# One change in three stages of a twelve-stage decoder: order of the expert choice, engine of the rounding, layout of the head transfers

## The chip, the cores and the metric

The kernel runs on one core of a Trainium2 chip, as one program. The metric is device time in microseconds (us). TensorE multiplies matrices, VectorE and ScalarE work elementwise, GpSimd does so too, SyncE issues the transfers between memory (HBM) and the on-chip SBUF; TensorE's results lie in PSUM. Each engine works through its own queue in order and waits for others on semaphores.

## The reference, cut to what matters

The residual `x` (2 batches of 512 tokens, 256 features) passes through twelve sublayers, each `x = x + f(layernorm(x))`. The change touches three of them:

```python
# L0_ffn: six experts e, 100 low-rank tokens each; every input token takes one expert
logits = x @ w_gate;  gates = one_hot(argmax(logits))          # top-1, softmax of one value = 1
attn   = softmax(x @ tokens[e].T / 16)                         # per expert, over its 100 tokens
delta  = ((attn[:, :, 1:] @ val[e, 1:] + x) @ wd_w.T + wd_b) * scale
out    = log(sum_e exp(delta) * gates)                         # 0 replaced by float32 eps

# L1_ffn: both matrix products on values rounded to whole numbers
q(x) = round(x / s),  s = max(|x|.max(), 1e-6) / 127
h = gelu((q(x) @ q(w1).T + b1) * s_x * s_w1);   out = (q(h) @ q(w2).T + b2) * s_h * s_w2

# L2_xattn: 16 heads of 16 features, 512 queries, 1024 keys per batch
p = softmax(q @ k.T / 4 + (1 - mask) * -1e9) * group_prob;   out = (p @ v) @ wo + bo
```

## The kernel before

Activations lie feature-major: 256 features as two chunks of 128 partitions, 1024 tokens along the free dimension. `decoder` calls the stages one after another with a fence between them: every engine's queue must be drained before the next stage starts. Within a stage the order on each engine is written out by hand in functions `tensor`, `scalar`, `vector`, `gpsimd` and `sync`, and a `Signal` is a semaphore count (`x(n)`: the n-th event of that name). `k.beat` (L157) issues filler matmuls whose results nobody reads.

**`l0_ffn`** (L701). Six value blocks are computed (L745, L846) and row 0 of `val` is cleared (L848), which leaves token 0 out. Then come eight tiles of 128 tokens. For a tile TensorE computes the scores of all six experts and the gate logits into one of two PSUM slots (L758). VectorE takes the maxima and finds the one chosen expert, ties by rank (L856 to L868); ScalarE does six exponentials with sums (L812); VectorE divides by the sum and by the choice (L870 to L874: reciprocal, times choice, times the 128x600 probabilities); TensorE transposes six blocks (L772) and ScalarE copies them out (L817). TensorE's order is: logits of tile `it`, then transposes of tile `it - 1`; for `it = 8` in place of logits the mixing of the first half (`mix`, L789). After the tiles follow `blend` (L889), `close` (L797) and `finish` (L896 to L901) per half. GpSimd adds the normed input to the residual once per half (L906).

**`l1_ffn`** (L1380). After eight GELUs (L1440) VectorE has eight per-partition maxima; `Quantizer` reduces them on VectorE (L1157), over the partitions by a GpSimd all-reduce (L1161), and forms scale and inverse (L1165, L1167). Rounding is by adding and subtracting 1.5 times 2 to the 23rd: the multiplication with the addition is on VectorE (L1478, a ring of four buffers), the subtraction, which also converts to bf16, on VectorE for even and on GpSimd for odd blocks (L1486, L1502). TensorE multiplies block by block (L1425), behind 12 filler matmuls. GpSimd adds the bias to the residual (L1506) and VectorE the scaled product (L1491).

**`l2_xattn`** (L1846). Queries and keys are split into three bf16 parts of falling size, and the score is one matmul with 96 rows: six products of parts times 16 features (L1989). A chunk of 128 features x 512 tokens (8 heads) is computed (L1951), split (L2070, L2074, L2153, L2255, L2157) and stored to a scratch tensor (L1915); `fetch` brings a head back with its 96 rows. The first six chunks have a buffer each; the six later ones, of heads 8 to 15, are made during the head loop and share one buffer, so ScalarE's split waits until the chunk before is stored. Before the loop SyncE issues: mask and group probabilities of batch 0 (2 MB each), chunks 0 to 2, a wait, head 0 for batch 0, chunks 3 to 5, a wait, head 0 for batch 1, mask and group of batch 1, head 1. The loop has 128 tiles (head, batch, 128 queries), four per head and batch, software-pipelined over steps: score, masked sum with negation and minimum (L2219), exponential (L2111), transposes (L2000), weighting by the group probabilities (L2231 and L2267), product with the values (L2011, L2015). ScalarE turns the integer mask into a float bias (L2080) in one operation per batch, that of batch 1 ahead of the exponential of tile 2.

```python
sp.dma_start(qs[z][blk * dh:(blk + n) * dh, q],
             scr_q[head][:, 0:n, q].rearrange("f j t -> j f t")).then_inc(*done.up())   # n = 3, 2, 1
```

Of the kernel before, what the change touches and what calls it, by code (L numbers as in the profile page):

```python
# [7 lines left out]
ACT = mybir.ActivationFunctionType  # L8
# [9 lines left out]
P = 128  # L18
# [682 lines left out]
def l0_ffn(k):  # L701
# [22 lines left out]
    (x_early,) = k.signals("pool", 1)  # L724

    def tensor(pe):
# [20 lines left out]
        for it in range(TILES + 1):  # L747
# [13 lines left out]
            else:  # L761
                pe.wait_ge(*exped(6 * TILES - 6))
                mix(pe, 0)
# [72 lines left out]
    def vector(dve):  # L836
# [10 lines left out]
        dve.wait_ge(*value_out(E_))  # L847
        dve.memset(val[0:1], 0.0).then_inc(*value_out.up())  # L848
        ln.scale(dve, 1)
        for it in range(TILES):  # L850
            ps, s, p = k.slot(2 + it % 2), sm[it % 2], prob3[it % 2]
            mx, ng, su, gr = s[:, 0:7], s[:, 8:14], s[:, 16:22], s[:, 24:30]
            eq, m2, rs = s[:, 32:38], s[:, 40:41], s[:, 48:54]
            gl = ps[:, S + L_:S + L_ + E_]
            dve.wait_ge(*logit(it + 1))
            dve.tensor_reduce(mx[:, 0:5], ps[:, 0:500].rearrange("p (e l) -> p e l", e=5), AX.X,  # L856
                              OP.max).then_inc(*pick.up())
            dve.tensor_reduce(mx[:, 5:6], ps[:, S:S + L_], AX.X, OP.max).then_inc(*pick.up())
            dve.tensor_reduce(mx[:, 6:7], gl, AX.X, OP.max).then_inc(*pick.up())
            dve.wait_ge(*pick(8 * it + 3))  # L860
            dve.tensor_scalar(ng, mx[:, 0:6], -1.0 / 16, None, OP.mult).then_inc(*pick.up())
            dve.tensor_scalar(eq, gl, mx[:, 6:7], None, OP.is_equal).then_inc(*pick.up())
            dve.wait_ge(*pick(8 * it + 5))
            dve.tensor_tensor(eq, eq, rank, OP.mult).then_inc(*pick.up())
            dve.wait_ge(*pick(8 * it + 6))
            dve.tensor_reduce(m2, eq, AX.X, OP.max).then_inc(*pick.up())
            dve.wait_ge(*pick(8 * it + 7))
            dve.tensor_scalar(eq, eq, m2, None, OP.is_equal).then_inc(*pick.up())  # L868
            dve.wait_ge(*exped(6 * it + 6))
            dve.reciprocal(rs, su).then_inc(*weighed.up())  # L870
            dve.wait_ge(*weighed(3 * it + 1))
            dve.tensor_tensor(gr, rs, eq, OP.mult).then_inc(*weighed.up())
            dve.wait_ge(*weighed(3 * it + 2))
            dve.tensor_tensor(p, p, gr.unsqueeze(2).broadcast_to([P, E_, L_]), OP.mult).then_inc(*weighed.up())  # L874
            if it == TILES - 1:
                blend(dve, 0)
# [7 lines left out]
        if nxt:  # L884
            nxt.scale(dve, 0)

# [16 lines left out]
    def gpsimd(pool):  # L903
        for h in range(B):
            pool.wait_ge(*ln.out(h + 1))
            pool.tensor_tensor(k.X[:, :, half(h)], k.X[:, :, half(h)], k.Hn[:, :, half(h)], OP.add).then_inc(*x_early.up())  # L906
# [473 lines left out]
def l1_ffn(k):  # L1380
# [17 lines left out]
    up, down = k.signals("pe", 2)  # L1398
    (gelu,) = k.signals("act", 1)
    bias1, largest, whole, scaled1, bias2, scaled, rounded_dve, resid = k.signals("dve", 8)  # L1400
    rounded_pool, x_early = k.signals("pool", 2)
# [3 lines left out]
    on_pool = lambda kt: kt % 2 == 1  # L1405
    rounded = lambda kt: (rounded_pool if on_pool(kt) else rounded_dve)(kt // 2 + 1)
# [4 lines left out]
    def tensor(pe):  # L1411
# [8 lines left out]
        k.beat(k.slot(2)[:, 0:S], 12)  # L1420
# [12 lines left out]
    def scalar(act):  # L1433
# [8 lines left out]
        act.preload_act_table_set(LN_EXP)  # L1442
        if nxt:
            nxt.square(act, 0)

    def vector(dve):
        ln.open_vector(dve)
# [25 lines left out]
        hid_q.scale(dve)  # L1473
        for kt in range(FC + 1):
# [9 lines left out]
            if kt and not on_pool(kt - 1):  # L1484
                dve.wait_ge(*scaled(kt))
                dve.tensor_scalar(hidq[:, kt - 1, :], tmp2(kt - 1), ROUND, None, OP.subtract).then_inc(*rounded_dve.up())  # L1486
# [10 lines left out]
    def gpsimd(pool):  # L1497
        in_q.gpsimd(pool)
        hid_q.gpsimd(pool)
        for kt in range(1, FC, 2):  # L1500
            pool.wait_ge(*scaled(kt + 1))
            pool.tensor_scalar(hidq[:, kt, :], tmp2(kt), 1.0, -ROUND, OP.mult, OP.add).then_inc(*rounded_pool.up())  # L1502
            if kt == 1:
                pool.wait_ge(*bias2(2))
            if kt in (1, 3):
                pool.tensor_scalar(k.X[:, kt // 2, :], k.X[:, kt // 2, :], 1.0, b2s[:, kt // 2:kt // 2 + 1], OP.mult,  # L1506
                                   OP.add).then_inc(*x_early.up())
# [338 lines left out]
def l2_xattn(k):  # L1846
    a, w, name, dh = k.a, k.work, "L2_xattn", 16
    NK, nk, keys, ROWS = B * S2, S2 // P, S2, 96
    scr_q = k.nc.dram_tensor("parts_q_" + name, (H, dh, 3, NT), BF16, kind="Internal").ap()
    scr_k = k.nc.dram_tensor("parts_k_" + name, (H, dh, 3, NK), BF16, kind="Internal").ap()  # L1850
# [27 lines left out]
    RING = (0, 1, 2, 4, 6)  # L1878
    count = lambda x, which: sum(ch[0] == which for ch in CHUNKS[:x])
# [23 lines left out]
    def fetch(sp, head, q, t, done):  # L1903
        z = head % 2
# [13 lines left out]
    def sync(sp):  # L1918
# [17 lines left out]
        for head in range(2, H):  # L1936
# [3 lines left out]
            if head == 8:  # L1940
                sp.wait_ge(*stored(len(CHUNKS)))
# [1480 lines left out]
```

## Time and profile before

| | us |
|---|---|
| median of 3 runs | 1848.98 (1846.49 to 1850.38) |
| profiled execution | 1846.75 |
| its span | 1845.4 |
| mean granted TensorE clock | 0.971 |

| engine | busy us | share |
|---|---|---|
| TensorE | 1658.8 | 90% |
| VectorE | 1052.5 | 57% |
| ScalarE | 905.1 | 49% |
| GpSimd | 428.8 | 23% |

The span is that of one profiled execution; times in the rows are microseconds from its start. On that scale `l0_ffn` lies at about 268 to 363, `l1_ffn` at 590 to 643 and `l2_xattn` at 985 to 1340. PE is TensorE, DVE VectorE, ACT ScalarE, POOL GpSimd, SP SyncE. L874 is line 874 of the kernel. A clock of 1.00 is 2.4 GHz and 0.50 is 1.2 GHz.

### The profile page before, as it was taken

The numbers are of one execution on the slowest core, as the hardware profiler recorded it, in microseconds if no ns is written. First come the engines' busy times: TensorE is split into PE (matmuls) and PEld (weight loads), VectorE is DVE, ScalarE is ACT, GpSimd is POOL, SyncE is SP. The second block draws the span as 40 slices with busy tenths as digits, with TensorE's granted clock in tenths as the row PEclk, the third lists the DMA queues.
The fourth block names the chain that finished last, engine by engine and source line by source line (L and its number), as shares of the span: only waits on it lengthen the run. The fifth ranks groups of instructions, "written<-read, shape, count | busy, mean of one in ns | idle before, by whom it ended". The sixth has DMA issues, their size and how long they took to land. (4 is left out here: it accounts for less than half of the span.)

```text
span 1845.4 us, 22986 instructions
## 1 busy us (share of the span) xinstructions
PE 1658.8 (90%) x7762; PEld 854.0 (46%) x7762; DVE 1052.5 (57%) x2163; ACT 905.1 (49%) x1762; POOL 428.8 (23%) x534
## 2 busy tenths in 40 slices
PE   7899997988998788999989689999988889999997
PEld 2334444434665234434335455566534444555545
DVE  4731115484322749889845578888737634655525
ACT  2331213352333247777833578878732563555523
POOL 0010000000000225555511345555601011232300
PEclk9999998999999899999999799999999899999999
DMA  5000100001000000000104311010116402000000
GB/s 220 1 0 0 40 0 1 33 2 46 1 1 17 1 9 9 18 10 10 50 1 149 132 52 51 33 37 29 31 41 178 132 8 85 21 11 21 1 1 23
DMA packets 31844, 69.42 MB, mean 38 GB/s; under 512 B 4213, under 2 KB 18357, under 8 KB 30293
## 3 DMA queue, kind: packets, MB, share of 16 engines
q1 hardware_dynamic: 31728, 67.95, 11.4%
q8 instruction: 63, 1.03, 0.2%
q14 instruction: 53, 0.43, 0.1%
HBM read 55.78 MB, written 12.06 MB: 37 GB/s over the span
## 5 line engine op out<-in xcount | busy, mean ns | idle before, releaser
L2267 POOL TENSOR_TENSOR work<-work,arena_a 128x512 f32<-128x512 f32 x128 | 167.9, 1312 | 155.8 <-ACT work L2129 155.5
L2000 PE MATMUL ps<-identity,ctx_keys 128*128 128x128 f32 x1024 | 144.9, 281 | 17.0 <-ACT work L2129 14.5
L2219 DVE CUSTOM_DVE_ANT_0 ctx_keys<-ps,arena_b 128x1024 f32<-128x1024 f32 x128 | 154.9, 1212 | 6.7 <-ACT arena_b L2080 6.2
L2000 PEld LDWEIGHTS ps<-identity,ctx_keys 128*128 128x128 f32 x1024 | 118.8, 144 | 65.3 <-ACT work L2129 21.3
L2111 ACT ACTIVATE ctx_keys<-ctx_keys,small 128x1024 f32<-128x1024 f32 x128 | 146.9, 1147 | 0.7 <-DVE small L2219 0.7
L2231 DVE TENSOR_TENSOR work<-ps,arena_a 128x512 f32<-128x512 f32 x128 | 88.0, 688 | 46.2 <-PE ps L2000 39.1
L3113 POOL TENSOR_SCALAR ctx_keys<-ctx_keys,small 128x128 f32<-128x128 f32 (+3 forms) x128 | 66.9, 535 | 172.6 <-DVE small L3036 172.6
L2129 ACT ACTIVATE work<-ps 128x512 f32<-128x512 f32 x128 | 76.3, 596 | 62.0 <-PE ps L2000 58.7
L1802 POOL TENSOR_SCALAR work<-work 128x1024 f32<-128x1024 int32 x64 | 66.6, 1040 | 112.7 <-DVE work L1755 112.3
L339 PE MATMUL ps<-work,arena_a 128*128 128x512 f32 x192 | 85.1, 595 | 7.9 <-DVE work L515 3.2
L1989 PE MATMUL ps<-work 96*128 96x512 bf16 x256 | 79.3, 393 | 14.2 <-DMA work<-parts_k_L_xattn 9.4
L214 ACT ACTIVATE norm_parts<-normed 128x1024 f32<-128x1024 f32 x24 | 25.3, 1054 | 129.2 <-DVE normed L207 129.2
L1601 PE MATMUL ps<-work 64*128 64x512 f32 x256 | 73.2, 648 | 16.7 <-DVE work L1755 14.5
L157 PE MATMUL ps<-identity 128*128 128x512 bf16 x320 | 79.5, 399 | 7.9 <-DVE normed L237 2.9
L2988 ACT ACTIVATE ctx_keys<-ctx_keys,small 128x128 f32<-128x128 f32 (+3 forms) x128 | 70.7, 553 | 29.1 <-DVE small L3028 28.7
L1755 DVE SCALAR_TENSOR_TENSOR work<-work,ps 128x1024 int32<-128x1024 f32 x64 | 78.0, 1218 | 12.2 <-ACT work L1693 12.1
L1738 DVE TENSOR_SCALAR work<-work,small 128x512 int16<-128x512 f32 x128 | 81.0, 674 | 2.3
L1677 ACT ACTIVATE work<-work 128x512 f32<-128x512 f32 x128 | 80.3, 644 | 2.4 <-POOL work L1802 2.4
L1161 POOL PARTITION_ALL_REDUCE small<-small x4 | 1.4, 358 | 328.7 <-DVE small L1157 328.7
L3062 DVE COPY work<-ps 128x128 f32<-128x128 f32 (+1 forms) x64 | 31.3, 489 | 75.7 <-PE ps L2904 75.2
L1625 PE MATMUL ps<-arena_a,work 128*64 128x512 f32 x256 | 66.3, 622 | 1.6 <-DVE work L1773 1.5
L1647 PE MATMUL ps<-normed,head_weights 128*128 128x512 f32 x128 | 63.7, 620 | 3.8 <-DVE work L1746 3.0
(389 smaller groups left out, 3417.3 us busy)
## 6 DMA issues: line engine op xcount, KB each, us to landing
arena_b<-in_mask SPq DMA_DIRECT2D x2, 2048.0 KB, 8.8
arena_a<-in_groupT SPq DMA_DIRECT2D x2, 2048.0 KB, 14.8
head_weights<-in_w_L_xattn SPq DMA_DIRECT2D x8, 449.0 KB, 3.3
arena_a<-in_w_l_attn SPq DMA_DIRECT2D x1, 3072.0 KB, 14.6
head_weights<-in_w_L_attn SPq DMA_DIRECT2D x8, 384.0 KB, 3.0
work<-parts_q_L_attn SPq DMA_DIRECT2D x8, 384.0 KB, 4.7
work<-parts_k_L_attn SPq DMA_DIRECT2D x8, 384.0 KB, 5.1
work<-parts_k_L_xattn SPq DMA_DIRECT2D x15, 192.0 KB
```

The source lines that it names most:

```text
L157: self.pe.matmul(bank, ib[:, 0:P], ib.unsqueeze(1).broadcast_to([P, 2, 2 * P]), start=True, stop=True)
L339: mm = pe.matmul(k.bank(i), wT[:, c, m * P:(m + 1) * P], src[:, c, :], start=c == 0, stop=c == DC - 1)
L1677: op = act.activation(ex[i % NE][:, h, :], ex[i % NE][:, h, :], ACT.Exp, scale=1.0 / FX, accum_out=sums[i % 4][:, h:h + 1])
L1738: op = dve.tensor_scalar(attn[i % 2][:, h * S:(h + 1) * S], ex[i % NE][:, h, :], recip[i % 4][:, h:h + 1], OFFSET - HALF, OP.mult, OP.add)
L1755: dve.scalar_tensor_tensor(out=score[i % NS], in0=sign[i % 2], scalar=-HALF, in1=s_bank[i % 2], op0=OP.mult, op1=OP.add).then_inc(*truncat ...
L1989: mm = pe.matmul(s_psum[i % NS][:, o:o + S], qs[h][0:ROWS, q0:q0 + P], ks[h][0:ROWS, b * keys + o:b * keys + o + S], start=True, stop=True)
L2000: mm = pe.transpose(t_psum[z][:, kt * P:(kt + 1) * P], prob[i % NP][:, o:o + P], k.iden[:, :])
L2111: act.activation(p, p, ACT.Exp, scale=-1.0, bias=minmax[:, i % 8:i % 8 + 1], accum_out=sums[:, i % 8:i % 8 + 1]).then_inc(*exped.up())
L2129: act.activation(PT[i // 4 % 2][:, 4:8, i % 4 * P:(i % 4 + 1) * P], t_psum[1].rearrange("p (k t) -> p k t", t=P), ACT.Copy).then_inc(*turn ...
L2219: dve.tensor_tensor_reduce(prob[i % NP], s_psum[i % NS], NEG[:, b, qt, :], -1.0, BIG * 3e8, OP.add, OP.min, minmax[:, i % 8:i % 8 + 1]).th ...
L2231: dve.tensor_tensor(PT[i // 4 % 2][:, 0:4, qt * P:(qt + 1) * P], t_psum[0].rearrange("p (k t) -> p k t", t=P), GT[:, b, 0:4, qt * P:(qt + ...
L2267: pool.tensor_tensor(p, p, GT[:, b, 4:8, qt * P:(qt + 1) * P], OP.mult).then_inc(*weighed_pool.up())
```

## The change

In `l0_ffn` the loop on VectorE is split into `choose` and `weigh`; `choose` of a tile is issued before `weigh` of the tile before, the second scale of the layernorm comes after the first `choose`, and the memset of the values' first row moves to GpSimd, between its two additions. TensorE waits for that memset before its first mixing; else its order is the same.

```diff
-        dve.wait_ge(*value_out(E_))
-        dve.memset(val[0:1], 0.0).then_inc(*value_out.up())
-        ln.scale(dve, 1)
-        for it in range(TILES):
...
+        for it in range(TILES + 1):
+            if it < TILES:
+                choose(dve, it)
+            if it == 0:
+                ln.scale(dve, 1)
+            if it:
+                weigh(dve, it - 1)
+        blend(dve, 0)
```

`choose` holds the operations L856 to L868, with the negation (L861) ahead of the gate's maximum (L859) and a wait of its own; `weigh` holds L870 to L874.

In `l1_ffn` the maximum over the partitions of the second quantization goes through TensorE: a transposition of the 128x1 maxima to one row, a reduction on VectorE, a matmul with a row of ones that brings it back to all partitions. Of the eight subtractions ScalarE gets six (blocks 1 to 3 and 5 to 7) and VectorE two; GpSimd keeps the two bias additions alone.

```diff
-        k.beat(k.slot(2)[:, 0:S], 12)
+        pe.wait_ge(*fixed(2))
+        k.beat(k.slot(2)[:, 0:S], 6)
+        pe.wait_ge(*hid_q.done(1))
+        pe.transpose(k.slot(0)[0:1, 0:P], hid_q.am, k.iden[:, :]).then_inc(*peak.up())
+        pe.wait_ge(*hid_q.done(2))
+        pe.matmul(k.slot(1)[:, 0:1], ones, top, start=True, stop=True).then_inc(*peak.up())
+        k.beat(k.slot(2)[:, 0:S], 5)
...
+        for kt in range(FC):
+            if on_act(kt):
+                act.wait_ge(*scaled(kt + 1))
+                act.activation(hidq[:, kt, :], tmp2(kt), ACT.Identity, bias=unround).then_inc(*rounded_act.up())
```

In `l2_xattn` the scratch tensors hold the six blocks of 128 partitions already repeated, with the features of the eight heads interleaved (the weights are laid out so on the host). A chunk is stored in three transfers, which together write six blocks; a head is fetched in two transfers of 96 rows each. The mask of batch 1 is turned in four pieces, at steps 3 to 6, ahead of the exponentials of tiles 1 to 4, and each masked sum waits for its own piece.

```diff
-        for blk, n in ((0, 3), (3, 2), (5, 1)):
-            sp.dma_start(qs[z][blk * dh:(blk + n) * dh, q],
-                         scr_q[head][:, 0:n, q].rearrange("f j t -> j f t")).then_inc(*done.up())
...
+        for dst, scr, tokens in ((qs, scr_q, q), (ks, scr_k, t)):
+            sp.dma_start(dst[z][0:ROWS, tokens],
+                         scr[m].rearrange("j (f h) t -> (j f) h t", h=8)[:, h, tokens]).then_inc(*done.up())
...
+    PIECES = {"q": (range(0, 3), range(0, 2), range(0, 1)), "k": ((0, 0, 0), (1, 1), (2,))}
+        for block in PIECES[which]:
+            n, j = len(block), block[0]
+            src = parts[x][:, 0:n, :] if which == "q" else parts[x][:, j:j + 1, :].broadcast_to([P, n, S])
+            sp.dma_start(scr[row:row + n, :, t0:t0 + S].rearrange("j p t -> p j t"), src).then_inc(*stored.up())
+            row += n
...
-            if step == 4:
-                mask(1)
+            if 3 <= step < 7:
+                mask(1, slice(step - 3, step - 2))
```

## Rows read from the trace of the kernel before

**Rows 1.** The page's busy times: us, share of the span, instructions.
```profile
PE 1658.8 (90%) x7762; PEld 854.0 (46%) x7762; DVE 1052.5 (57%) x2163; ACT 905.1 (49%) x1762; POOL 428.8 (23%) x534
```
**Rows 2.** Order of time, VectorE, one tile of `l0_ffn`: start, duration, operation.
```profile
304.34 0.67 DVE L856 TENSOR_REDUCE small<-ps 128x5 f32<-128x500 f32 x1
...
306.01 0.23 DVE L868 TENSOR_SCALAR small<-small 128x6 f32<-128x6 f32 x1
308.37 0.19 DVE L870 RECIPROCAL small<-small 128x6 f32<-128x6 f32 x1 [2.13 <-ACT work L812]
...
308.80 0.78 DVE L874 TENSOR_TENSOR work<-work,small 128x600 f32<-128x600 f32 x1
309.50 0.67 DVE L856 TENSOR_REDUCE small<-ps 128x5 f32<-128x500 f32 x1
```
**Rows 3.** Order of time, TensorE in `l0_ffn`: transposes, logits, mixing.
```profile
294.25 1.49 PE L772 MATMUL ps<-identity,work 128*100 128x128 f32 x6 [5.80 <-DVE work L874]
...
305.24 2.27 PE L758 MATMUL ps<-arena_b,normed 128*128 128x500 f32 x8
309.72 0.83 PE L772 MATMUL ps<-identity,work 128*100 128x128 f32 x6 [2.22 <-DVE work L874]
310.39 3.87 PE L758 MATMUL ps<-arena_b,normed 128*128 128x500 f32 x8
...
325.87 10.46 PE L789 MATMUL ps<-work,arena_b 100*128 100x512 f32 x24
```
**Rows 4.** Order of time around the first tile of `l0_ffn`, GpSimd and VectorE.
```profile
287.62 2.34 POOL L906 TENSOR_TENSOR resid<-resid,normed 128x1024 f32<-128x1024 f32 x1 [14.31 <-DVE normed L237]
...
288.40 1.58 DVE L861 TENSOR_SCALAR small<-small 128x6 f32<-128x6 f32 x1
...
293.32 0.78 DVE L874 TENSOR_TENSOR work<-work,small 128x600 f32<-128x600 f32 x1
```
**Rows 5.** Stretch, length, busy us of the five engines, granted clock, DMA share, GB/s.
```profile
309.50:314.70 5.20, 4.54 (x14) 2.60 (x14) 2.87 (x13) 2.76 (x13) 0.00 (x0) 0.67 0.02 5
```
**Rows 6.** Order of time in `l1_ffn` from the last GELU to the residual.
```profile
618.14 4.40 PE L157 MATMUL ps<-identity 128*128 128x512 bf16 x12 [2.45 <-ACT work L1440]
...
620.56 1.42 DVE L1478 TENSOR_SCALAR arena_b<-work,small 128x1024 f32<-128x1024 f32 x2
...
627.93 1.03 POOL L1502 TENSOR_SCALAR work<-arena_b 128x1024 bf16<-128x1024 f32 x1 [7.79 <-issue]
...
630.55 1.52 DVE L1486 TENSOR_SCALAR work<-arena_b 128x1024 bf16<-128x1024 f32 x1
...
635.12 1.41 POOL L1502 TENSOR_SCALAR work<-arena_b 128x1024 bf16<-128x1024 f32 x1 [0.64 <-DVE arena_b L1478]
...
637.32 2.73 DVE L1491 SCALAR_TENSOR_TENSOR resid<-ps,small,resid 128x512 f32<-128x512 f32 x4 [1.68 <-PE ps L1425]
```
**Rows 7.** The page's groups, ScalarE on 128x1024: busy us, mean ns.
```profile
L1693 ACT ACTIVATE work<-ps 128x1024 f32<-128x1024 f32 x64 | 65.7, 1026 | 0.0
```
**Rows 8.** Order of time at the start of `l2_xattn`'s loop: SyncE, ScalarE, TensorE.
```profile
1014.36 1.91 SPq L1906 DMA_DIRECT2D work<-parts_q_L_xattn  x3
...
1018.20 0.41 SPq L1922 DMA_DIRECT2D arena_b<-in_mask  x1
...
1028.19 3.71 ACT L2080 ACTIVATE arena_b<-arena_b,small 128x4096 f32<-128x4096 int32 x1 [10.88 <-DMA arena_b<-in_mask]
...
1041.81 1.03 PE L1989 MATMUL ps<-work 96*128 96x512 bf16 x2 [2.86 <-DMA work<-parts_k_L_xattn]
...
1045.08 1.14 ACT L2111 ACTIVATE ctx_keys<-ctx_keys,small 128x1024 f32<-128x1024 f32 x1
```
**Rows 9.** Stretches as in Rows 5: masks in flight, then a head's fetch alone.
```profile
1024.00:1027.00 3.00, 3.00 (x13) 2.44 (x12) 0.69 (x1) 0.00 (x0) 0.00 (x0) 0.50 1.02 403
1036.00:1039.00 3.00, 2.95 (x16) 2.17 (x14) 2.36 (x6) 2.16 (x5) 1.73 (x2) 0.68 0.17 68
```
**Rows 10.** Waits in `l2_xattn`: who for whom, us in total, times, longest.
```profile
ACT head_weights L2074 <- DMA parts_k_L_xattn<-head_weights: 0.8, 1, 0.8
```

More of the change, by code:

```diff
@@ L1397, in l1_ffn @@
     in_q, hid_q = Quantizer(k, view(k.small, 8, 4)), Quantizer(k, view(k.small, 12, 4))
-    up, down = k.signals("pe", 2)
-    (gelu,) = k.signals("act", 1)
+    up, down, peak = k.signals("pe", 3)
+    gelu, rounded_act = k.signals("act", 2)
     bias1, largest, whole, scaled1, bias2, scaled, rounded_dve, resid = k.signals("dve", 8)
-    rounded_pool, x_early = k.signals("pool", 2)
+    (x_early,) = k.signals("pool", 1)
+    (fixed,) = k.signals("dve", 1)
+    ones, top, unround = view(w, 0, P)[0:1], view(k.small, 17, 1)[0:1], view(k.small, 16, 1)
     hv = hq.rearrange("p (c t) -> p c t", c=2)
@@ L1446, in vector @@
     def vector(dve):
+        dve.memset(unround, -ROUND).then_inc(*fixed.up())
+        dve.memset(ones, 1.0).then_inc(*fixed.up())
         ln.open_vector(dve)
@@ L1472, in vector @@
         hid_q.largest(dve, am8)
-        hid_q.scale(dve)
+        dve.wait_ge(*peak(1))
+        dve.tensor_reduce(top, k.slot(0)[0:1, 0:P], AX.X, OP.max).then_inc(*hid_q.done.up())
+        dve.wait_ge(*peak(2))
+        dve.tensor_scalar(hid_q.s, k.slot(1)[:, 0:1], 1e-6, 1.0 / 127, OP.max, OP.mult).then_inc(*hid_q.done.up())
+        dve.wait_ge(*hid_q.done(3))
+        dve.reciprocal(hid_q.inv, hid_q.s).then_inc(*hid_q.done.up())
+        dve.wait_ge(*hid_q.done(4))
         for kt in range(FC + 1):
@@ L1483, in vector @@
                 dve.tensor_scalar(b2s, k.vec[:, col:col + 2], ss[:, 1:2], None, OP.mult).then_inc(*bias2.up())
-            if kt and not on_pool(kt - 1):
+            if kt and not on_act(kt - 1):
                 dve.wait_ge(*scaled(kt))
@@ L1498, in gpsimd @@
         in_q.gpsimd(pool)
[L1499 to L1507, printed above, removed]
+        pool.wait_ge(*bias2(2))
+        for c in range(DC):
+            pool.tensor_scalar(k.X[:, c, :], k.X[:, c, :], 1.0, b2s[:, c:c + 1], OP.mult, OP.add).then_inc(*x_early.up())
     sync(k.sp)
@@ L1914, in store @@
         sp.wait_ge(*low(x + 1))
-        sp.dma_start((scr_q if which == "q" else scr_k)[8 * m:8 * m + 8, :, :, t0:t0 + S].rearrange(
-            "h f j t -> (h f) j t"), parts[x]).then_inc(*stored.up())
+        scr, row = (scr_q if which == "q" else scr_k)[m], 0
+        for block in PIECES[which]:
[3 more added lines that the diff above has]
+            row += n
     def sync(sp):
@@ L2072, in split, with mask @@
             if x > NF:
-                act.wait_ge(*stored(x))
+                act.wait_ge(*stored(3 * x))
             act.activation(parts[x][:, 0, :], rest[x][0], ACT.Copy).then_inc(*hi.up())
-        def mask(b):
-            flat = NEG[:, b].rearrange("p q k -> p (q k)")
+        def mask(b, tiles):
+            flat = NEG[:, b, tiles].rearrange("p q k -> p (q k)")
             act.wait_ge(*mask_in[b](1))
@@ L2088, in scalar @@
             if y == 4:
-                mask(0)
+                mask(0, slice(0, 4))
         act.wait_ge(*zeroed(2))
@@ L3355, in lay_out @@
             ws, bs = list(ws), list(bs)
-            for j in range(2 if n == "L3_attn" else 0):
+            for j in range(2):
                 ws[j] = ws[j].reshape(D, DC, 8, 16).transpose(0, 1, 3, 2).reshape(D, D)
```

91 lines of the change are left out of this document (47 added, 44 removed).

## The prediction, made from the rows above

> **What bounds the kernel now.** I read the busy shares first: TensorE is busy 90% of the span [rows 1], so the twelve stages are mostly its chain, and an edit can move the time only in stretches where TensorE stands. The chain of waits covers the last stage alone; the three stretches touched were therefore read from the order of time of each engine. All three have gaps on TensorE, so each can give or take.
>
> In `l0_ffn` eight tiles of 128 tokens go round VectorE (choose), ScalarE (exponentials), VectorE (weigh), TensorE (transposes). The round is 5.16 us, from the reduction at 304.34 to the next at 309.50. In it VectorE chooses for 1.90 us (304.34 to 306.24), waits 2.13 for ScalarE, and weighs [rows 2]. TensorE's logits for the tile after are done in that wait, and cost nothing now. After the last round TensorE mixes for 10.46 us [rows 3], and works on nearly without a gap to the end of the stage: what the rounds lose, the stage loses.
>
> In `l1_ffn` the second whole-number rounding stands on GpSimd: its first rounding begins at 627.93 after 7.79 us in which the engine waited for nothing visible. In `l2_xattn` TensorE stands before tile 4 and, 2.86 us, before tile 8 for transfers, and ScalarE 10.88 us for the second batch's mask [rows 8].
>
> **The change part by part.** *Experts.* VectorE now chooses tile i+1 before it weighs tile i, which hides the exponentials. But TensorE's order is as before: logits of tile i+1, transposes of tile i, logits of tile i+2. So choosing i+2 needs its logits, these stand behind the transposes of tile i, and those need weighing of i. The round becomes weigh, transpose, logits, choose. Start of the last weighing operation to start of the transposes 0.92 (308.80 to 309.72, the latter the next such row), transposes to logits 0.67, logits 2.27 [rows 2, 3], choosing 2.01 (1.90, and 0.11 since the negation now follows straight on the reduction it reads), reciprocal to last weighing operation 0.43 (308.37 to 308.80), less 0.04 for overlaps and wake-ups: 6.26 us at the full clock, 1.10 more than before. Between tile 0's and tile 6's weighing lie six rounds: 6.6 us. Tile 7 needs no further logits, and its transposes stand behind the mixing, so it adds nothing. TensorE's new wait for the zeroed row stands before the mixing, 35 us after GpSimd clears it: nothing.
>
> The first weighing was at 293.32 [rows 4]. The memset of one partition leaves VectorE and choice 0 starts a scale earlier, but a second choice now comes before it, and a small VectorE operation took 1.58 instead of 0.17 while GpSimd added at 287.62 [rows 4]. GpSimd's own new memset is not in the trace: between nothing (it runs beside) and that same 2.34. Clean, the first weighing comes at 291.8, with one such block at 294.2; I take 293.5, +0.2, nearer the blocked end since GpSimd's work falls on choice 1.
>
> The clock: three of seven rounds had logits at about half speed, as 3.87 us instead of 2.27 [rows 3], with a granted 0.67 [rows 5]; 1.6 us more each, hidden then behind 2.2 us of standing. Now the logits are on the path and TensorE stands 3.3 us of each round. With half to all of the six rounds slowed: 4.8 to 9.6; with none: 0. I take three, 4.8. Stage: 6.6 + 0.2 + 4.8 = +11.6 (5 to 17).
>
> The Trainium skill, "TensorE: Matmul & The Clock Gate", Part 1, says that an idle stretch puts the engine back to 1.2 GHz and that sustained work releases it. The rows agree: the transposes at 294.25, behind 5.80 us of standing, took 1.49 instead of 0.83 [rows 3]. Read strictly, it would slow every round, which is a rival below.
>
> *Rounding.* Before, from the first multiplication at 620.56 to the first addition to the residual at 637.32 it was 16.8 us, with the standing for GpSimd inside [rows 6]. Now the largest value goes through TensorE: its transposition stands behind six filler matmuls, which began at 618.14 and at 12 in 4.40, the first ones at 0.43, end at about 620.7. Then transposition 0.4, reduction 0.3, a one-column matmul 0.4, two small VectorE operations 0.4: first multiplication at 622.3, 1.7 later. (Bounds of the two unseen matmuls: nothing and 0.83 as for six transposes [rows 3].) VectorE has eight multiplications of 0.71 (two in 1.42) and two roundings of 0.68; GpSimd's two additions, released at 624.0, block it meanwhile as at 630.55, where one took 1.52 [rows 6]: +1.5. ScalarE has six roundings; the nearest row is a 128x1024 activation, 1.03 [rows 7]. It ends last: VectorE's last but two multiplications at 628.9, three roundings behind it with their waits, 632.6. The old last rounding on GpSimd ended at 636.53 and the addition began 0.79 later; so now 633.4. That is -3.9 (-5.2 without blocking, -2.5 with the half clock and dearer roundings). GpSimd's silent 7.8 us comes now after the first all-reduce, whose result the first matrix product needs, and is over long before 618; if it began only with the bias, the additions would end at 634.5, and the gain were 1 to 2 less. Behind the two new waits of TensorE stand five filler matmuls and the product, which wait for VectorE anyway. Two memsets at the start: 0.1.
>
> *Attention: transfers.* A head's blocks came in six transfers over rows of 3, 2 and 1 outer steps: 68 GB/s against 403 for the masks with 128 rows [rows 9]. Now two transfers with 96 rows each; I take the mask's rate, bounded by 68. Tile 4 needs the fetch issued at 1014.36, tile 8 the one behind the second mask. For this each chunk is stored six times over instead of three, in three transfers. Three chunks: 1.18 MB more, 2.9 us at the masks' 403 GB/s; a store's runs are shorter, so I take 3.5. So SyncE's first wait ends at 1006.6 instead of 1003.1, its six plus three stores last to 1012.5, and the second wait ends near 1017.5 instead of 1014.36. The fetch then issues in 1.2 instead of 3.8, and the mask goes out at 1019 instead of 1018.20. It took 10.0 to land (1018.20 to 1028.19 [rows 8]) among narrow fetches; its 2 MB alone take 5.2 at 403 GB/s. Between these I take 8.3: 1027.3, 1 us sooner.
>
> *Attention: mask in pieces.* ScalarE turned the second mask in one 3.71 us operation at 1028.19 [rows 8]; now in four of 0.93 between exponentials, the first ahead of exponential 1, so that one exponential (1.13) moves behind the landing. VectorE can take tile 4 after one piece. Counting on from 1027.3 on ScalarE (four pieces 3.7, exponentials at 1.13, copies at 0.6), exponential 7 starts at 1041.8. Before it started at 1045.08 [rows 8], after tile 8's wait to 1041.81, which falls away. -3.3; bounds 0 (the mask lands as late as before and a piece waits on something else) and -12 (the whole of the stall from 1017 to 1045 that eight exponentials at 2.0 don't fill).
>
> *Attention: later chunks.* They share one buffer: a chunk's split waits until the one before is stored. Once this already cost ScalarE 0.8 [rows 10]. Doubled bytes cost 1 us each, the wide fetches no longer crowd them: 0 to 1 for each of five. I take 0.3, +1.5. If each such stop also drops the clock, at the 1.6 us that a slow round of the experts shows, it is up to 2.4 each, 12.
>
> The Trainium skill, "DMA: Bandwidth & Descriptors", section on why a DMA increments its semaphore by 16, has the number of engines as the largest up to 16 that divides the outermost dimension of both sides: 3, 2 and 1 before, 16 now. The trace agrees for the old ones (0.17 of 16 engines busy), and a head's 0.58 MB would by it take some 1.5 us.
>
> **Sum.** 11.6 - 3.9 + 0.1 - 3.3 + 1.5 = +6.0 on the profiled execution's 1846.75: 1852.8. Its time lies 2.2 below the median of the runs shown, 1848.98, and 1.35 above its span. Against the median: 1855.0; I put the time between, nearer the median: 1854.5.
>
> **The rivals.** (a) *The restart of the attention decides.* The whole stall of 12 us goes, since both waits for transfers and the mask are one knot. 11.6 - 3.9 - 12 + 1.5 = -2.8: 1846, not slower. It decides from a gain of 8 us in that stretch. For: waits of 10.9 and 2.9 us in one stretch of 30 [rows 8]. Against: the mask's 2 MB and the doubled stores stay in front. (b) *The clock stays down in the experts' rounds.* At half speed, transposes to logits take 1.3 and logits 4.4: round 8.9, six of them +22.6 instead of 11.4, total +17: 1866. The clock rule of the Trainium skill, named above, would give this if read strictly. For: 3.3 us of standing each round. Against: at a slow round TensorE works over 5 us, which has brought it back each time. (c) *The stores' wait*: 12 instead of 1.5, total +16.5: 1865. (d) *It does as it says*: choosing ahead shortens the round to VectorE's own 3.1, 12 us saved: -18, 1831. Against: it needs tile i+2's logits before tile i's transposes, and the order of TensorE's queue has them after.
>
> **How the numbers follow.** Forecast 0.56 (own range 1849 to 1861), (a) 0.17, (b) 0.11, (c) 0.07, (d) 0.09, in which any part of that saving is counted. 0.2% is 3.7 us, about what a measurement of this kernel tells from no change. The forecast lies above that in 0.42 and within in 0.14; (a) is within in 0.12, faster in 0.05. Slower 0.42 + 0.11 + 0.07 = 0.60; same 0.26; faster 0.05 + 0.09 = 0.14. The range leaves out (d), a part of (b) and of (a)'s fast end: 1845 to 1865.
>
> **What would show it.** The round of the experts: the five-way reductions spaced 6.3 us or more, TensorE waiting for VectorE before the transposes and VectorE for TensorE's logits; a spacing under 5.2 refutes the main term. First multiplication in `l1_ffn` near 622.3 on the old scale, the residual addition 15.2 us after the last GELU instead of 19.2. In the attention the second mask landing 9 to 10 us after tile 3's score, exponential 7 3 us sooner against tile 0's score, no DMA wait at tile 8, and ScalarE waiting for stores up to five times. A granted clock of 1.0 through the rounds would bring it to 1850.

## The result, and the profile after

| | before | after |
|---|---|---|
| median, us | 1848.45 (1840.14 to 1855.52, 16 runs) | 1856.09 (1850.30 to 1862.87, 16 runs) |
| ratio | | 1.0045, 95% interval 1.0028 to 1.0062 |
| profiled execution's span, us | 1845.4 | 1856.8 |
| mean granted TensorE clock | 0.971 | 0.964 |

The change is slower, by 7.6 us in the medians and 11.4 in the two profiled spans. The forecast was 1854.5. The shares on the page of the kernel after barely moved against [rows 1]: TensorE is busy 13.5 us longer with the same count of instructions (a few of them are others, since `l1_ffn` swaps filler matmuls), so a good part of the loss is like work done slower.

```profile
PE 1672.3 (90%) x7762; PEld 861.6 (46%) x7764; DVE 1050.6 (57%) x2163; ACT 912.8 (49%) x1771; POOL 424.7 (23%) x530
```

**`l0_ffn`.** VectorE's order of time, one round in the kernel after. Choosing begins at 309.83, the weighing's last step follows at 312.19 with no wait for ScalarE (the 2.13 us of [rows 2] are gone), but the next choice waits 5.82 us for TensorE's logits. The round is 8.96 us where [rows 2] has 5.16.

```profile
309.83 0.68 DVE L871 TENSOR_REDUCE small<-ps 128x5 f32<-128x500 f32 x1 [4.59 <-PE ps L758]
...
311.77 0.18 DVE L890 RECIPROCAL small<-small 128x6 f32<-128x6 f32 x1
...
312.19 0.78 DVE L894 TENSOR_TENSOR work<-work,small 128x600 f32<-128x600 f32 x1
318.79 0.68 DVE L871 TENSOR_REDUCE small<-ps 128x5 f32<-128x500 f32 x1 [5.82 <-PE ps L758]
```

TensorE in the same stage: before each block of transposes but the first it stands 3.33 us, the transposes take 1.49 or 1.40 instead of the 0.83 of [rows 3], and the logits 4.35 and 3.30 in turn instead of the 2.27 of a round at full clock. The first mixing block behind the loop, 10.46 in [rows 3], takes 12.72.

```profile
313.12 1.49 PE L773 MATMUL ps<-identity,work 128*100 128x128 f32 x6 [3.33 <-DVE work L894]
314.40 4.35 PE L758 MATMUL ps<-arena_b,normed 128*128 128x500 f32 x8
322.08 1.49 PE L773 MATMUL ps<-identity,work 128*100 128x128 f32 x6 [3.33 <-DVE work L894]
323.37 3.30 PE L758 MATMUL ps<-arena_b,normed 128*128 128x500 f32 x8
...
348.22 12.72 PE L790 MATMUL ps<-work,arena_b 100*128 100x512 f32 x24
```

Two consecutive rounds as stretches (columns as in [rows 5], whose slow round had a clock of 0.67): the clock is down for a part of every round now.

```profile
309.80:318.80 9.00, 5.63 (x14) 3.40 (x14) 2.91 (x12) 2.87 (x13) 0.00 (x0) 0.62 0.00 0
318.80:326.70 7.90, 4.58 (x14) 2.90 (x14) 2.90 (x11) 2.87 (x13) 0.00 (x0) 0.78 0.00 1
```

The first tile: GpSimd's new memset, then its addition, and the VectorE step that they block.

```profile
290.82 1.37 POOL L917 MEMSET arena_b<- 1x1536 f32 x1 [16.34 <-DVE normed L237]
...
291.55 2.97 DVE L875 TENSOR_SCALAR small<-small 128x6 f32<-128x6 f32 x1
292.16 2.33 POOL L918 TENSOR_TENSOR resid<-resid,normed 128x1024 f32<-128x1024 f32 x1
...
295.83 0.78 DVE L894 TENSOR_TENSOR work<-work,small 128x600 f32<-128x600 f32 x1
```

**`l1_ffn`**, order of time from the last GELU (its end, 641.35) to the residual. Against [rows 6]: first multiplication 3.16 us behind the GELU's end (2.45 before), ScalarE's first rounding at 645.96, and the addition to the residual at 655.40, 14.05 us behind the end of the GELU instead of 19.2.

```profile
641.39 1.47 PE L157 MATMUL ps<-identity 128*128 128x512 bf16 x6 [2.98 <-ACT work L1460]
...
643.06 0.27 PE L1437 MATMUL ps<-identity,small 128*1 128x128 f32 x1 [0.20 <-DVE small L1169]
...
643.70 0.38 PE L1439 MATMUL ps<-small,work 1*128 1x1 f32 x2 [0.37 <-DVE small L1500]
...
644.51 1.42 DVE L1510 TENSOR_SCALAR arena_b<-work,small 128x1024 f32<-128x1024 f32 x2
...
645.96 1.15 ACT L1466 ACTIVATE work<-arena_b,small 128x1024 bf16<-128x1024 f32 x1 [3.32 <-DVE arena_b L1510]
...
655.40 0.75 DVE L1523 SCALAR_TENSOR_TENSOR resid<-ps,small,resid 128x512 f32<-128x512 f32 x1 [2.34 <-PE ps L1445]
```

**`l2_xattn`.** The first masked sum stands at 1013.72 before and 1031.69 after; times here are best read from it. Against [rows 8] the mask is 4.5 us nearer to it on ScalarE (10.0 instead of 14.5), tile 4 waits 1.74 us for its transfer, tile 8 for none, and the exponential of tile 7 comes 23.7 us behind the first masked sum instead of 31.4.

```profile
1034.16 0.43 SPq L1950 DMA_DIRECT2D arena_b<-in_mask  x1
...
1036.41 1.03 PE L2017 MATMUL ps<-work 96*128 96x512 bf16 x2 [1.74 <-DMA work<-parts_k_L_xattn]
...
1041.70 1.15 ACT L2108 ACTIVATE arena_b<-arena_b,small 128x1024 f32<-128x1024 int32 x1 [7.56 <-DMA arena_b<-in_mask]
...
1055.36 1.15 ACT L2139 ACTIVATE ctx_keys<-ctx_keys,small 128x1024 f32<-128x1024 f32 x1
```

### The profile page after: what moved, and what is told of

The parts are those of the page before. It is cut to its first block and busy times, and to the rows that moved or that the text cites. A ratio compares the mean times of both kernels' runs of the same rounds, so it can differ in the third digit from the quotient of the medians.

```text
span 1856.8 us, 22958 instructions
## 1 busy us (share of the span) xinstructions
PE 1672.3 (90%) x7762; PEld 861.6 (46%) x7764; DVE 1050.6 (57%) x2163; ACT 912.8 (49%) x1771; POOL 424.7 (23%) x530
## 3 DMA queue, kind: packets, MB, share of 16 engines
q8 instruction: 63, 1.03, 0.2%
## 5 line engine op out<-in xcount | busy, mean ns | idle before, releaser
L1627 PE MATMUL ps<-work 64*128 64x512 f32 x256 | 73.2, 648 | 16.7 <-DVE work L1781 14.5
```

## The experiments

The theory: the whole loss is in `l0_ffn`, where VectorE's order closes a chain through TensorE once a tile and the standing halves TensorE's clock; the other two edits gain. The rivals: the order alone, without the clock; the new memset on GpSimd; a part of the loss in the doubled stores. "The ledger" in the expectations is the comparison of the two profiled executions stage by stage. Ratios are to the kernel before as it ran beside each kernel, with 95% intervals.

| kernel | median, us | ratio |
|---|---|---|
| experts' edit alone | 1868.44 | 1.0105 (1.0091 to 1.0120) |
| the change without it | 1838.08 | 0.9947 (0.9935 to 0.9959) |
| the change, weighing first again | 1837.82 | 0.9940 (0.9926 to 0.9954) |
| the change, idle multiplications | 1847.43 | 0.9990 (0.9977 to 1.0003) |
| the change, logits a tile ahead | 1829.99 | 0.9905 (0.9885 to 0.9926) |
| the same, idle multiplications | 1825.36 | 0.9882 (0.9859 to 0.9904) |
| experts as before, idle multiplications | 1838.64 | 0.9949 (0.9932 to 0.9965) |
| rounding's edit alone | 1844.26 | 0.9984 (0.9969 to 0.9999) |
| transfers' edit alone | 1839.92 | 0.9959 (0.9943 to 0.9974) |
| the same, six fetches a head | 1845.95 | 0.9984 (0.9967 to 1.0002) |
| mask in pieces alone | 1848.13 | 0.9998 (0.9986 to 1.0010) |

### Where the loss is: the experts' edit alone, and all but it

The first has of the diff only the part in `l0_ffn`, the second all but that part.

> Of the change only the expert stage's edit (choose one tile ahead, the silent vector on GpSimd). Theory: that stage alone carries the whole loss, and more: 23 us longer as in the changed kernel's trace, rounds of 7.8 and 9.0 us in turn, 1848.5 + 23 = 1871.5. Rival, the sum of the prediction for this stage (+11.6): 1860. Rival, the loss in this stage is in part made by what the other two edits left in memory or in the queues: under 1858.

> The change without the expert stage's edit: the whole-number rounding and the two-transfer attention alone. Theory by the ledger of the two traces (-6.5 and -7.1): 1835, and the expert stage as before, rounds of 5.2 us. Rival, the prediction's own sums for these two (-3.9 and -1.8): 1843. Rival, the two gains are given back at the end of the attention: 1848.

Measured 1868.44 and 1838.08: 20.2 us above and 10.2 below the kernel before of the same runs, 1848.25. The two theories by the ledger stand, each some 3 us too large (1871.5 and 1835 were expected), and the sums of the prediction for both are too small. Of the experts' edit alone, the six rounds between the first weighing and the seventh lasted 46.9 us (294.39 to 341.25), against 50.2 in the kernel after (295.83 to 346.00) and 30.9 before; one of them ran at the full clock and lasted 6.27, behind the same 3.33 us of standing as the others. So the clock's share differs from execution to execution. So does the first mixing block behind the loop: it took 12.16 us in four of six traces of kernels that have the experts' stage of before with nothing added (10.46 in the other two, the kernel before among them), and 10.46 in the trace of the experts' edit alone. The kernel before's row is that of a quick case.

```profile
329.06 12.16 PE L789 MATMUL ps<-work,arena_b 100*128 100x512 f32 x24
```

The row is of the kernel without the experts' edit.

### VectorE's order undone

```diff
-            if it < TILES:
-                choose(dve, it)
             if it == 0:
                 ln.scale(dve, 1)
             if it:
                 weigh(dve, it - 1)
+            if it < TILES:
+                choose(dve, it)
```

> The changed kernel with one thing undone: VectorE weighs the last tile before it chooses the next one's experts, as before; the silent vector stays on GpSimd, the two reductions keep their new order. Theory (VectorE's order alone makes the stage long): rounds of 5.2 us, the transposes at full speed in most, 1836. Rival (the vector on GpSimd, which TensorE's and VectorE's first steps wait for or share a port with): no more than 3 us of the 23 come back there, 1853.

The second scale of the layernorm is back ahead of the first `choose` with it. 1837.82: the order of the calls on VectorE is worth 18 us in the medians, the whole loss and more. In the order of time of this kernel, VectorE again waits 2.13 us for ScalarE (the row of [rows 2]) and the round is 5.29.

```profile
310.13 0.19 DVE L890 RECIPROCAL small<-small 128x6 f32<-128x6 f32 x1 [2.13 <-ACT work L813]
...
315.42 0.19 DVE L890 RECIPROCAL small<-small 128x6 f32<-128x6 f32 x1 [2.13 <-ACT work L813]
```

The memset on GpSimd and the helper functions, which stay in, cost nothing that can be measured in this order of VectorE. What the memset costs in the new order is not separated: no run has the new order with the memset on VectorE.

### The clock's share: idle multiplications before the transposes

```diff
+                for _ in range(18):
+                    pe.matmul(k.slot(j % 2)[:, 768:1024], ib[:, 0:P], ib, start=True, stop=True)
                 pe.wait_ge(*weighed(3 * j + 3))
```

> The changed kernel with 18 idle multiplications of 256 columns before each tile's transpositions, to fill the 3.3 us in which TensorE waits for the weighing. Theory (of the 23 us only 7 to 9 are the new order, the rest the half clock that the standing brings): granted clock near 1 in the loop, transposes 0.83 instead of 1.49, rounds of 6.3 us, 1856 - 8 x 2.0 = 1840. Rival (the chain of waits alone sets the round and the clock is only a sign of it): rounds stay at 8.3, 1856, or longer where the multiplications push the transposes back, 1860.

1847.43, 8.7 us less than the kernel after (10 by the ratios): the clock's theory stands, with about half of the 16 us that it put on it. Its TensorE rows: 18 idle multiplications fill 2.13 of the 3.33 us of standing, the transposes take 0.86, the logits blocks 2.27, and the round is 6.21 us (start to start of the transposes). This holds from the second round on; in the first the transposes took 1.52, the logits 3.72 and the round 8.3.

```profile
309.38 2.13 PE L773 MATMUL ps<-identity 128*128 128x256 bf16 x18
312.79 0.86 PE L776 MATMUL ps<-identity,work 128*100 128x128 f32 x6 [1.27 <-DVE work L897]
313.48 2.27 PE L758 MATMUL ps<-arena_b,normed 128*128 128x500 f32 x8
...
318.99 0.87 PE L776 MATMUL ps<-identity,work 128*100 128x128 f32 x6 [1.27 <-DVE work L897]
```

The stretch in the columns of [rows 5]:

```profile
314.00:320.00 6.00, 4.73 (x33) 3.46 (x32) 2.90 (x11) 2.63 (x14) 0.00 (x0) 1.00 0.00 0
```

The order alone is worth 6.21 - 5.16 = 1.05 us a round, 6.3 for six. The rest is the clock: in the profiled execution of the kernel after 12.9 us of its rounds, and 2.3 of the mixing behind them if that counts (above). From the last value addition to the last addition to the residual the stage takes 98.8 us in the kernel after, 86.0 with the idle multiplications, 92.6 in the trace of the experts' edit alone, 75.4 before. The 12.8 us between the first two are more than the 8.7 to 10 of the medians. The 6 us between the kernel after and the experts' edit alone, which have the same code in this stage, show that one trace of the kernel after is not its median. The idle multiplications cost something themselves too: behind the first mixing block, where TensorE has no gap to fill, they put the next block about 1 us later (12.9 us from start to start instead of 11.9 before).

The Trainium skill, "TensorE: Matmul & The Clock Gate", Part 1, says that idle puts the engine back to 1.2 GHz and that sustained work releases it. The trace agrees: with the work put back, 1.00; without it, 0.62 and 0.78. The one round at full clock of the experts' edit alone, behind 3.33 us of standing, is an exception to reading it as "every round".

### The same multiplications where the logits aren't on the path

The experts' stage of before, with 10 of them a tile; the other two edits stay in.

> The other two edits alone with the expert stage as before, and 10 idle multiplications of 256 columns before each tile's transpositions. Theory (in the order of before the logits end 0.6 us before the transposes may start even at half speed, so the clock costs next to nothing in the loop): rounds stay at 5.2, 1838, with up to 2 us from the first tile and the mixing behind the loop. Rival (the clock alone explains what the loop costs): rounds under 5, 1834 or less.

1838.64 against 1838.08 without them. TensorE ran at full speed (logits 2.27 in every round shown, with 3.86 and 3.94 in the kernel without them) and the round stayed at 5.16 (311.04 to 316.20). Here a slow clock in the loop costs nothing, because nobody waits for the logits. The up to 2 us from the first tile and the mixing did not show in the median, though the stage was 2.4 us shorter in this trace (75.4 against 77.8).

```profile
311.04 0.86 PE L775 MATMUL ps<-identity,work 128*100 128x128 f32 x6 [1.10 <-DVE work L877]
311.74 2.27 PE L758 MATMUL ps<-arena_b,normed 128*128 128x500 f32 x8
...
316.20 0.87 PE L775 MATMUL ps<-identity,work 128*100 128x128 f32 x6 [1.10 <-DVE work L877]
```

### TensorE's order too: the logits a tile ahead

A third logits slot (the transposes share one); TensorE issues the logits of tile i+2 ahead of the transposes of tile i.

```diff
-                if it >= 2:
-                    pe.wait_ge(*exped(6 * (it - 1)))
+                if it >= 3:
+                    pe.wait_ge(*exped(6 * (it - 2)))
...
-                ps = k.slot(2 + it % 2)
+                ps = k.slot((2, 3, 0)[it % 3])
...
-            if it:
-                j = it - 1
+            if it >= 2:
+                j = it - 2
```

> The changed kernel, but TensorE computes each tile's logits one tile ahead too (a third logits buffer; the transpositions share one), so that choosing the next tile's experts waits for nothing that the weighing needs. Theory (choosing first costs only because the logits come late): VectorE's eleven steps of a tile take 3.15 us, TensorE's transposes and logits 0.83 + 2.27, so the round falls to 3.3 to 3.8 at full clock, below the 5.2 before the change; with the other two edits 1838 - 7 x 1.6 = 1827. Rival (the chain through exponentials and transposes still closes once a tile): rounds of 5.2, 1838. Rival (clock stays at half in the denser loop): transposes and logits 1.49 + 4.3, rounds of 5.8, 1843.

1829.99. The VectorE order that cost 18 us now gains: the ratio is 0.9905 against 0.9940 with both old orders, some 6.5 us, between intervals that just touch. From 305.22 to 308.42 is 3.20 us, then 3.06, with no wait on VectorE, a little under the 3.3 to 3.8 expected, and TensorE's logits stay at 2.27 in all rounds but the first (3.95). TensorE's new order with VectorE's old one was not run; that it gains nothing by itself is argued from the rows, where the logits were not waited for.

```profile
305.22 0.67 DVE L870 TENSOR_REDUCE small<-ps 128x5 f32<-128x500 f32 x1
...
307.57 0.78 DVE L893 TENSOR_TENSOR work<-work,small 128x600 f32<-128x600 f32 x1
308.42 0.68 DVE L870 TENSOR_REDUCE small<-ps 128x5 f32<-128x500 f32 x1
...
310.78 0.78 DVE L893 TENSOR_TENSOR work<-work,small 128x600 f32<-128x600 f32 x1
311.48 0.67 DVE L870 TENSOR_REDUCE small<-ps 128x5 f32<-128x500 f32 x1
```

With 12 idle multiplications before tile 0's transposes and 14 before tile 6's:

> The kernel with the logits a tile ahead, and idle multiplications of 256 columns at the two places where TensorE still stands in this stage: 12 before the first tile's transpositions (5.0 us standing), 14 before the last but one's (2.4 us). Theory (the clock pays wherever TensorE sets the pace next): the first transposes 0.83 instead of 1.49, the logits behind them 2.3 instead of 3.95, the first mixing block 10.5 instead of 12.1, up to 4.0 in all: 1826 to 1828. Rival (these are hidden behind VectorE, or the clock falls whatever is done here): 1830.

1825.36, the fastest kernel of this study, 1.2% under the kernel before. The six rounds take 18.8 us instead of 21.1, since the first one is at the full clock too, and the first mixing block is back at 10.47 (12.13 without), a value that it also had in some kernels without such help. That these last 4.6 us are the idle multiplications' is likely but not sure: the two intervals overlap.

```profile
314.91 10.47 PE L794 MATMUL ps<-work,arena_b 100*128 100x512 f32 x24
```

### The rounding alone

> Of the change only the whole-number rounding. Theory by the ledger (-6.5, all of it in this stage): 1842. Rival, the prediction's -3.9: 1844.5. Rival (the expert stage's edit made the ledger's number larger than it is): above 1846.

1844.26, -2.9 in its own runs (interval -5.7 to -0.2). The prediction's -3.9 lies within, the ledger's -6.5 outside: the two profiled executions differ in this stage by more than the edit. Ahead of the last GELU, where the change adds two small memsets and nothing else, the stage took 23.0 us before, 21.6 in the kernel after and, in other traces, 21.1 to 23.1 (from the first reduction of the layernorm's output); the interval behind it was 18.5 in the traces with the transfers' edit alone and the mask's alone, where the rounding is that of before, against 19.2 before. In its trace the residual's addition comes 14.0 us behind the last GELU's end, as in the kernel after. In the kernel without the experts' edit it came 15.1 behind: there the six filler matmuls ran slow, 2.74 us, and held the transposition:

```profile
623.23 2.74 PE L157 MATMUL ps<-identity 128*128 128x512 bf16 x6 [2.46 <-ACT work L1448]
625.77 0.42 PE L1425 MATMUL ps<-identity,small 128*1 128x128 f32 x1
```

### The attention's three parts

Transfers' edit alone, mask pieces alone, and the new layout with three fetches each for q and k:

```diff
-            sp.dma_start(dst[z][0:ROWS, tokens], scr[m]...[:, h, tokens])
+            for blk, n in ((0, 3), (3, 2), (5, 1)):
+                sp.dma_start(dst[z][blk * dh:(blk + n) * dh, tokens], scr[m][blk:blk + n]...[:, h, tokens])
```

> Of the change only the attention's stores and fetches (nine pieces stored, a head fetched in two transfers); the mask's second half is still one piece on ScalarE, waited for in whole. Theory: the mask lands 4.5 us sooner, the first tile of its half is still held by the 3.7 us piece, so 3 to 4 of the 7 us: 1845. Rival (all of the gain is the transfers): 1841. Rival (stores of twice the bytes give it back): 1849 or more.

> Of the change only the mask's second half in four pieces on ScalarE, each tile waiting for its own; transfers as before. Theory: the mask lands at 42.6 of the stage as before and the pieces wait for it in front of the exponential of tile 1, 3 to 4 us of work sooner than the whole did: nothing gained or up to 3 lost, 1848 to 1851. Rival, the prediction's (the exponential of tile 7 comes 3.3 sooner by the pieces alone): 1846.

> Of the change only the new layout with its doubled stores; a head is fetched in six transfers again (three blocks of q, three of k), mask in one piece. Theory (the gain comes from the number of transfers and SP's time to issue them, 3.7 to 10.5 us for six against 0.8 to 5.4 for two): the gain of the transfers goes, 1846 to 1848. Rival (the gain comes from the layout: the stores' shorter landing, 3.3 instead of 4.1 to 5.8 us, and the form of what is read): it stays, 1841.

1839.92, 1848.13 and 1845.95. The transfers are the gain (-7.5 by their ratio), the pieces nothing that can be measured, and six fetches a head give back some 60% of it, by ratios whose intervals overlap. Counted in each trace from the first masked sum:

| us | exponential 7 | exponential 9 | read-out of the last masked sum |
|---|---|---|---|
| before | 31.36 | 38.58 | 316.04 |
| transfers alone | 25.31 | 32.47 | 309.06 |
| the same, six fetches | 27.20 | 34.53 | 312.74 |
| mask in pieces alone | 29.63 | 37.91 | 316.22 |
| after | 23.67 | 30.77 | 309.01 |
| without the experts' edit | 24.38 | 31.49 | 306.55 |

The last two have the same code in this stage, so the last column is good to some 2.5 us, the other two to 0.7.

With the transfers alone, SyncE's rows: head 1's fetch is issued in 4.61 and 0.81 us behind the masks, where the kernel before took 7.34 and 3.19 for its three and three. But this is not the count of the issues: with six fetches in the new layout the three and three took 4.20 and 1.35, as long in all as the two (5.6 and 5.4 us). Two wide fetches took 3.6 us in the kernel after and 4.0 in the one without the experts' edit. So the long hold behind the masks goes with the old layout of the fetches, and which of its traits makes it is not shown. The stores, in three transfers each and twice the bytes, did not hold SyncE longer: with the transfers alone it waited for them 7.4 us in all before its fetches, 11.8 before.

```profile
1015.46 0.33 SPq L1907 DMA_DIRECT2D work<-parts_q_L_xattn  x1
1015.83 0.43 SPq L1907 DMA_DIRECT2D work<-parts_k_L_xattn  x1
1016.30 0.43 SPq L1924 DMA_DIRECT2D arena_b<-in_mask  x1
...
1017.32 4.61 SPq L1907 DMA_DIRECT2D work<-parts_q_L_xattn  x1
1021.97 0.81 SPq L1907 DMA_DIRECT2D work<-parts_k_L_xattn  x1
```

With six fetches:

```profile
1018.13 4.20 SPq L1908 DMA_DIRECT2D work<-parts_q_L_xattn  x3
...
1022.39 1.35 SPq L1908 DMA_DIRECT2D work<-parts_k_L_xattn  x3
```

What the count does cost stands ahead of the masks: each half of head 0 is issued in 2.6 us by six and in 0.8 by two, so the second mask goes out 6.0 us behind the first masked sum instead of 2.9, and ScalarE starts on it at 13.7 instead of 12.4 (14.5 before). That fits the 1.9 us of exponential 7; the further 1.7 by the end of the loop were not followed, and are within what the last column is good to.

TensorE's waits for these transfers, from the first masked sum to 1060, fall from 9.4 us in two to 2.1 in one (4.5 in one with six fetches); this is the row of the kernel with the transfers alone:

```profile
PE ps L1991 <- DMA work<-parts_k_L_xattn: 2.1, 1, 2.1
```

## Why the prediction was right

Sign and size held, 1856.09 in a range of 1845 to 1865, but partly by luck, by two errors that cancel: the experts' stage lost twice what was forecast, the attention gained four times.

*The order chain of `l0_ffn`: right.* Forecast 6.26 us a round at full clock; 6.21 with the idle multiplications, 6.27 in the one round of the experts' edit alone that had the full clock. VectorE waits for the logits, TensorE for the weighing, as named.

*The clock: mis-sized.* The step "With half to all of the six rounds slowed: 4.8 to 9.6; with none: 0. I take three, 4.8" was too small. In the kernel after all were slow, and not only by the logits' 1.6: the transposes' 0.5 to 0.6 count too. Rounds of 8.6, 7.7, 9.0, 7.9, 9.0 and 8.0 us make 50.2 against 37.6 forecast without the clock, so its term is 12.6 where 4.8 stood (9.3 in the trace of the experts' edit alone). 2.3 more stand at the mixing block, for which nothing was put down; but a slow first mixing block is in four of six traces with the old stage as well, so the new order isn't shown to be its cause. Rival (b), which gave +22.6 for six rounds of 8.9, had this nearer right (+19.2 measured). But not every round was slow in full, as it had it: they alternate. Its sentence "TensorE works over 5 us, which has brought it back each time" takes more from the rows of before than they show: over 5 us is a slow round of the new loop (5.63 us busy), one of before had 4.54 [rows 5]. And a slow round of before ate its own standing, 0.61 or 0.54 us in front of the next transposes instead of 2.22, while in the chain the standing is 3.33 whatever the logits take. Two rows of the kernel before, a full round behind 2.22 and the row behind a slow one:

```profile
304.57 0.83 PE L772 MATMUL ps<-identity,work 128*100 128x128 f32 x6 [2.22 <-DVE work L874]
...
314.88 0.83 PE L772 MATMUL ps<-identity,work 128*100 128x128 f32 x6 [0.61 <-DVE work L874]
```

In the kernel after the clock came back towards the end of a round's logits, was 1.00 while TensorE stood from 319 to 322, and 0.51 from 322 to 323, where the transposes begin.

*The first tile: +1.3 instead of +0.2.* Counted from the last value addition, the weighing comes 1.3 later. One block was forecast at up to 2.34; the memset's 1.37 and the addition stand one behind the other, and a step of 0.17 took 2.97, until the addition's end.

The stage in all: 19.2 + 0.6 (slow last transposes) + 2.3 + 1.3 = 23.4, and the landmarks of the two traces, from the stage's first matmul to the next stage's work, give 23.2. Forecast 11.6. By the medians the edit costs 18 to 20.

*The rounding: right in mechanism, small in size.* -3.9 forecast, -5.2 from GELU to residual in the kernel after, -2.9 (-0.2 to -5.7) in the median alone. The filler matmuls ran at the full clock and did not stand in front of the transposition; where they ran slow the interval was 15.1, and 15.2 was forecast. ScalarE's rounding takes 1.15 (1.03 taken). GpSimd's two additions blocked VectorE as forecast, by 1.5 us: four multiplications beside them took 4.37 where 2.84 is the free price. The fear of GpSimd's silent stretch did not come true.

*The attention: mis-sized, with the weights on the wrong step.* The forecast gave the gain to the pieces of the mask (-3.3) and a loss to the stores (+3.5 on the first wait, +1.5 for later chunks). In the kernel after the first wait ended 2.8 later in the stage, but the second, at 1033.32, only 1.0 later where 3.1 were forecast, for the three smaller stores land sooner than one (3.0 to 3.5 us from issue to landing, 4.1 and 5.8 before; the first three chunks, with the masks in flight, do not: up to 7.9 against 7.7), and ScalarE has no wait for stores in the loop. And the fetches in front of the mask take 0.8 us instead of 3.8. So the second mask went out 2.0 us earlier in the stage where 0.8 later was forecast, and ScalarE took it up 7.5 us later instead of 8.3. Head 1, behind the masks, was issued in 10.5 us before, 3.6 in the kernel after and 5.4 with the transfers alone; the forecast put no price on that. -7.0 in the traces by the transfers alone. Rival (a), the whole 12, did not come, but its point (the waits are one knot of transfers) was the better description; its threshold of a gain of 8 was nearly met.

One reading of a page is wrong there too. By the rule on the number of engines that the prediction takes from the Trainium skill, "DMA: Bandwidth & Descriptors", a block of one copy has its 16 features as the slowest dimension that is not of size 1, so the three kinds of fetch before would use 3, 2 and 16 engines, not 3, 2 and 1. The sum did not use it, and no row here shows the engines of a single fetch.

*Where the other 1.3 us of `l1_ffn` come from* by which the stage shortened beyond the 5.2: they lie ahead of the last GELU (21.6 us instead of 23.0). There the first product's 30 matmuls took 6.65 us at a granted 1.00, instead of 8.34 at 0.79. It was 6.65 and 1.00 with the transfers' edit alone too, which changes nothing in this stage, and 8.34 and 0.79 in the kernel without the experts' edit, which has the new rounding. So it is the clock of that execution, not the edit.

*Not shown:* how the clock's share spreads over many runs; only one execution of each kernel has a trace. Nor how much of the first tile's 1.3 us is the memset's.

## What to carry to other kernels

Before moving a step ahead on one engine, follow what it reads back through the other engines' queues: software pipelining on VectorE alone turned a hidden wait into a chain (+18 us), and the same order with TensorE's queue moved as well gained about 7. When a chain makes TensorE stand, price every matmul of the loop at half speed as the upper bound, and expect executions to differ; idle multiplications bring back the clock, but time only where TensorE is waited for. And price each transfer's issue on its queue by its form and by its place: here six instead of two ahead of the mask sent the mask out later, while behind the masks the form of the fetches counted and not their number.

## What the runs showed that was not expected

- Issuing is slow while masks load: three fetches of q took 7.34 us of SyncE before, three in the new layout 4.20, one 4.61 with the transfers alone and 2.74 in the kernel after; with free queues 0.6 to 0.7 each in the old form and 0.3 to 0.5 in the new. Doubling the stores' bytes in three transfers lost nothing.
- The half clock can touch every round of a loop: in the kernel after, rounds behind 3.33 us of standing had 0.62 or 0.78; in the experts' edit alone one of six had the full clock behind the same 3.33. Before, three rounds began behind 2.22 us; one ran at full clock and two were slow, and behind each slow one TensorE stood 0.61 or 0.54 us and the next was at full clock. With the 3.33 filled up to 1.27, all but the first were at full clock.
- A GpSimd memset on one partition (1x1536, 1.37 us) right ahead of a 2.33 us addition stretched one 0.17 us VectorE step to 2.97.
